# Four-block conditioned transformer stack: loops written out, and three small moves in the 16-head attention stages

## The chip, the cores and the metric

One NeuronCore of one Trainium2 chip runs the whole program, with one launch. The metric is the device time of an execution in microseconds (us); lower is better. The engines are named as in the profile: PE (TensorE, with PEld for its weight loads), DVE (VectorE), ACT (ScalarE), POOL (GpSimd) and SP (SyncE, which issues most DMAs).

## The reference

The input x has 64 sequences of 64 tokens with 256 features, 4096 tokens in all. Four blocks change it one after the other; each takes its shifts, scales and gates from a condition vector of the sequence. All is computed in fp32.

```python
# block 0: layer norm, 16 heads of 64, gelu MLP of 1024
# block 1: rms norm, 16 heads of 16 with q/k rms norm and 3-D rope, SwiGLU of 682
# block 2: layer norm, 16 heads of 16 with rope by position, gelu MLP, then a gate unit
# block 3: two low-rank products per sequence, with gelu between
h = norm(x) * (1 + scale_a) + shift_a
q, k, v = heads(h @ Wqkv)
q, k = rope(qk_norm(q), qk_norm(k))        # block 1; block 2 without the norm
x = x + gate_a * (softmax(q @ k.T / sqrt(d)) @ v @ Wo + bo)
h = norm(x) * (1 + scale_m) + shift_m
x = x + gate_m * mlp(h)
```

## The kernel before, in words

x stays in SBUF as X, features on the partitions. The tokens go through every stage in NCH = 8 chunks of 512. The stages, each a block of its own with a barrier at its end, are: attention0 (block 0, 64 features a head), feed_forward, attention12 (block 1), feed_forward, attention12 (block 2), feed_forward, the gate unit (feed_forward again, kind "gate") and low_rank.

A large product is three fp32r products (`split3`): the weights and the activations are each held as a rounded high half and the rest as a low half. For activations, ACT writes the high half HH from H32 (`act_hh`, line 298), and DVE the low half HL = H32 - HH (`dve_hl`, line 396). For weights of the next stage, ACT and mostly POOL do the same during the last two chunks (`wt.high`, `wt.low`, line 206; two pieces a step in attention12).

`Front` makes the normed and modulated chunk H32. In attention12 this runs ahead: in body c it works on chunk c + 2 (`early`). Its pieces there are: a square on ACT and a sum XS of it on POOL (`pool_ss`, line 314) in step 1; high and low part of that sum in step 2 (`act_sqh`; `pool_sql`, line 318, writes FB); variance on PE (`pe_var`, line 338, reads FB), its root and DVE's Newton steps in step 3, with POOL's scale and shift (`pool_h`, lines 325 and 332); the high half in the tail.

attention12 has no scheduler. The order of each engine is that of its own `step` function, called by `steps`: body c runs step t = 1, 2, 3 of chunk c and then step 0 of chunk c + 1 as its tail. A step handles 128 tokens, tile tt = 4c + t, and looks ahead: the projection to q and k is made for tile tt + 2 (`pe_proj`, line 1413), the rotation by POOL for tile tt + 2 (`pool_rope`, lines 1508 to 1513), the transposes of q and k for tile tt + 1 (`qk_t`, line 1556), the weighted sum for tile tt - 1. In block 1 the q/k norm lies between: ACT squares the projection (`act_square`, line 1435), DVE sums (`dve_sum`, line 1466), ACT takes the root (`act_root`, lines 1440 and 1442), DVE multiplies (`dve_qk`, line 1483). ACT also copies the transposed softmax weights out of two PSUM banks (lines 1686 to 1689, PT); the first of these banks is the one that `qk_t` writes next, so `qk_t` waits for the first copy.

Before the change, ACT takes the root of tile tt + 2 ahead of the two copies in steps 1, 2 and 3, and behind them in step 0 only. DVE makes the low half of chunk c + 1 in step 1 of body c, behind `spread_k` (line 1735); PE needs it in step 2, whose projection is the first of chunk c + 1. In body 0 (`lead`) the low half of chunk 1 stands at the end of step 1. The projected result is scaled by the gate into RT or RTa (line 1745), and POOL adds it to X two bodies later (`add`, line 1816), in the tail behind the rotation.

Loops: `chunks` runs bodies 0 to 5 as a hardware loop of three turns with two bodies each (line 441), the last two straight; `steps` of attention12 runs body 0 straight, 1 to 4 in a loop of two turns (line 1527), and 5 to 7 straight. The gate unit is straight already. In a loop, semaphore values and addresses that depend on c come from registers.

## Time and profile before

| | before |
|---|---|
| median of 3 runs | 2075.79 us (2071.45 to 2076.36) |
| profiled execution, its time | 2075.19 us |
| its span in the trace | 2073.4 us |
| mean granted TensorE clock | 0.968 |
| PE busy | 1872.6 us (90%) |
| DVE, ACT, POOL busy | 1380.5, 1028.9, 799.0 us |

The stages end at about 619.4, 836.1, 1150, 1380, 1670, 1880, 2036 and 2073.4 us of the span, in the order above. Busy time is time in which an instruction runs on the engine; waits and register instructions are not in it. The granted clock is a share of TensorE's full speed. In rows in order of time, "x2" is a row of two merged instructions, and a bracket gives the idle time of the engine before it and what ended it.

### The profile page before, as it was taken

The page shows a single profiled execution, that of the slowest core. Times are in us where ns is not written, and L with a number is a line of the kernel's source. Part 1 is how long each engine was busy: PE and PEld are TensorE (multiplying, and loading weights), DVE is VectorE, ACT ScalarE, POOL GpSimd, SP SyncE. Part 2 cuts the span into 40 slices and gives each one's busy share as a digit, 9 for nine tenths or more (in the row PEclk, how much of TensorE's full clock was granted, in tenths as well). Part 3 has the DMA queues.
Part 4 walks back from the last instruction along what each step waited for, and adds up shares of the span by engine and source line. Part 5 has one row for each costly group of instructions (what it writes and reads, how often), then busy time and mean ns, then how long its engine had stood idle before and what let it go on. Part 6 is the DMA issues. An engine that isn't in the chain of part 4 may idle for free. (4 is left out here: it accounts for less than half of the span.)

```text
span 2073.4 us, 42326 instructions
## 1 busy us (share of the span) xinstructions
PE 1872.6 (90%) x16038; PEld 1464.3 (71%) x16038; DVE 1380.5 (67%) x2128; ACT 1028.9 (50%) x1793; POOL 799.0 (39%) x737
## 2 busy tenths in 40 slices
PE   5999999999979998688988899978999889998998
PEld 4778777877867776466766677756777677776775
DVE  4665666566655665588898577767889756664555
ACT  3544444444447665366666344324555556663332
POOL 1210211021123445557668233446777824450000
PEclk8999999999989999799999999989999999999999
DMA  5100000000010000100000000010000000003322
GB/s 187 72 2 2 2 2 2 2 2 2 2 50 13 0 0 1 46 2 3 2 2 2 28 0 0 0 41 2 2 0 2 2 31 0 0 1 91 107 77 82
DMA packets 26596, 44.58 MB, mean 22 GB/s; under 512 B 4289, under 2 KB 12289, under 8 KB 26305
## 3 DMA queue, kind: packets, MB, share of 16 engines
q1 hardware_dynamic: 25152, 42.01, 6.1%
q8 instruction: 123, 2.02, 0.4%
q10 hardware_dynamic: 1280, 0.23, 0.1%
q14 instruction: 41, 0.33, 0.1%
HBM read 35.94 MB, written 6.29 MB: 20 GB/s over the span
## 5 line engine op out<-in xcount | busy, mean ns | idle before, releaser
L1230 DVE TENSOR_TENSOR Glb<-Gfb,Ghb 128x512 fp32r<-128x512 f32 x176 | 155.7, 894 | 67.0 <-ACT Ghb L1181 65.3
L449 PE MATMUL bank<-HH,W1b 128*128 128x512 f32 x448 | 184.8, 413 | 16.0 <-PEq L1538 7.1
L325 POOL TENSOR_TENSOR Tm<-Dv,MOD 128x512 f32<-128x512 f32 x94 | 108.4, 1173 | 204.6 <-DVE Dv L388 128.9
L451 PE MATMUL bank<-HH,W1b 128*128 128x512 f32 x448 | 177.2, 396 | 0.0
L450 PE MATMUL bank<-HL,W1b 128*128 128x512 f32 x448 | 177.0, 395 | 0.0
L449 PE MATMUL O<-Ghb,W2b 128*128 128x512 f32 x352 | 141.0, 400 | 31.7 <-DVE Glb L1230 31.6
L469 POOL TENSOR_TENSOR spare<-RT 128x1 f32<-128x1 f32 x32 | 11.4, 355 | 397.9 <-DVE RT L460 397.9
L314 POOL TENSOR_TENSOR XS<-Tm 128x512 f32<-128x512 f32 x48 | 70.1, 1460 | 214.5 <-ACT Tm L280 209.6
L451 PE MATMUL O<-Ghb,W2b 128*128 128x512 f32 x352 | 138.0, 392 | 0.0
L450 PE MATMUL O<-Glb,W2b 128*128 128x512 f32 x352 | 137.6, 391 | 0.0
L669 DVE COPY VP<-bank 64x256 f32<-64x256 f32 x128 | 54.0, 422 | 114.0 <-PE bank L632 112.7
L1413 PE MATMUL bank<-WQKa,HH 128*128 128x512 f32 x256 | 91.0, 438 | 41.0 <-DVE HL L396 17.9
L1689 ACT ACTIVATE PTa<-bank 128x512 f32<-128x512 f32 x128 | 69.4, 593 | 98.4 <-PE bank L1569 98.4
L449 PEld LDWEIGHTS bank<-HH,W1b 128*128 128x128 f32 x448 | 85.8, 191 | 41.4 <-issue 17.8
L1180 ACT ACTIVATE Gfb<-bank,bias_cols 128x512 f32<-128x512 f32 x128 | 88.0, 688 | 51.0 <-DVE Glb L1230 40.9
L449 PE MATMUL bank<-HH,WQK 128*128 128x512 f32 x256 | 107.4, 420 | 4.6 <-DVE HL L396 4.6
L449 PEld LDWEIGHTS O<-Ghb,W2b 128*128 128x128 f32 x352 | 66.3, 188 | 56.1 <-DVE Glb L1230 43.0
L332 POOL TENSOR_TENSOR H<-Tm,MOD 128x512 f32<-128x512 f32 x94 | 98.5, 1069 | 11.8 <-POOL Tm L325 10.6
L450 PE MATMUL bank<-HL,WQK 128*128 128x512 f32 x256 | 101.5, 396 | 0.0
L451 PE MATMUL bank<-HH,WQK 128*128 128x512 f32 x256 | 101.4, 396 | 0.0
L632 PE MATMUL bank<-WV,HH 128*128 128x256 f32 x512 | 98.7, 286 | 2.7 <-DVE WV L206 2.7
L450 PEld LDWEIGHTS bank<-HL,W1b 128*128 128x128 f32 x448 | 86.0, 192 | 20.8 <-issue 3.3
(266 smaller groups left out, 5278.2 us busy)
## 6 DMA issues: line engine op xcount, KB each, us to landing
w<-l_w_dram SPq DMA_DIRECT2D x33, 256.0 KB, 3.4
X<-xT_dram SPq DMA_DIRECT2D x16, 256.0 KB, 6.7
out_dram<-XO SPq DMA_DIRECT2D x8, 512.0 KB, 2.7
wm<-w_mods_dram SPq DMA_DIRECT2D x4, 768.0 KB, 5.0
W2b_f<-l_w_dram SPq DMA_DIRECT2D x11, 256.0 KB, 5.2
WQK_f<-l_wqk_dram SPq DMA_DIRECT2D x8, 256.0 KB, 7.3
W1b_0f<-l_w_dram SPq DMA_DIRECT2D x8, 256.0 KB, 3.6
wm<-w_mods_dram SPq DMA_DIRECT2D x4, 384.0 KB, 6.7
```

Of the source, the lines that this page charges most:

```text
L314: nc.gpsimd.tensor_tensor(XS[:], Tm[:, 0], Tm[:, 1], ALU.add).then_inc(f_ss.h, 1)
L325: nc.gpsimd.tensor_tensor(Tm[:, k].rearrange("p (b t) -> p b t", t=T), Dv[:, k].rearrange("p (b t) -> p b t", t=T), m, ALU.mult).then_inc( ...
L332: last = nc.gpsimd.tensor_tensor(H32[p][:, k].rearrange("p (b t) -> p b t", t=T), Tm[:, k].rearrange("p (b t) -> p b t", t=T), m, ALU.add)
L449: nc.tensor.matmul(out, w_lo_ap, x_hi, start=first, stop=False)
L450: nc.tensor.matmul(out, w_hi_ap, x_lo, start=False, stop=False)
L451: return nc.tensor.matmul(out, w_hi_ap, x_hi, start=False, stop=last)
L632: last = nc.tensor.matmul(out, (HH, HL)[xp][p][:, k, tok_], WV[wp][:, k, :, jj * DH0:(jj + 2) * DH0], start=(k == 0 and wp == 1), stop=(k ...
L669: last = nc.vector.tensor_copy(v_dst(jj, 1, a, b), v_src(1, a, b))
L1180: nc.scalar.activation(Gf[m % 2][:], src, ACT.Gelu, bias=bias(0, m))
L1230: nc.vector.tensor_tensor(Gl[m % gb][:], gf, Gh[m % gb][:].bitcast(F32), ALU.subtract).then_inc(g_lo.h, 1)
L1413: last = nc.tensor.matmul(QKB[:], (HH, HL)[xp][p][:, k, t * P:(t + 1) * P], WQK[wp][:, k], start=(i == 0 and k == 0), stop=(i == 2 and k = ...
L1689: nc.scalar.activation(PT[:, 4 * i:4 * i + 4].rearrange("p r q -> p (r q)"), bank[:], ACT.Copy).then_inc(pt_sb.h, 1)
```

## The change

It has four parts. (1) All loops are written out: `chunks` and `steps` no longer take the engine, and call the body eight times with constants. (2) In both attention12 stages the low half of a chunk is made by POOL, in the tail step, behind the rotation (`pool_hl`), from body 0 on for chunk c + 2; DVE keeps only the one of chunk 1 in body 0. (3) POOL's add to X moves from the tail to the next step, step 1, behind its rotation; only the add of the last tail stays. (4) In block 1 ACT takes the root in step 1 behind the two copies, as it did in step 0.

```diff
+            def pool_hl(self, pool, c, p):
+                pool.wait_ge(f_hh.h, self.at(f_hh, c + 1))
+                nc.gpsimd.tensor_tensor(HL[p][:], H32[p][:], HH[p][:].bitcast(F32), ALU.subtract).then_inc(f_hl.h, 1)
...
-        def chunks(eng, body, unrolled=False):
-
-            if unrolled:
-                for c in range(NCH):
-                    body(c, c % 2, 2 if c < NCH - 2 else NCH - 1 - c)
-                return
-            with eng.Fori(0, NCH // 2 - 1) as j:
-                body(2 * j, 0, 2)
-                body(2 * j + 1, 1, 2)
-            body(NCH - 2, 0, 1)
-            body(NCH - 1, 1, 0)
+        def chunks(body):
+
+            for c in range(NCH):
+                body(c, c % 2, 2 if c < NCH - 2 else NCH - 1 - c)
...
-                    body(0, 0, 2)
-                    with eng.Fori(0, NCH // 2 - 2) as j:
-                        body(2 * j + 1, 1, 2)
-                        body(2 * j + 2, 0, 2)
-                    body(NCH - 3, 1, 2)
-                    body(NCH - 2, 0, 1)
-                    body(NCH - 1, 1, 0)
+                    for c in range(NCH):
+                        body(c, c % 2, 2 if c < NCH - 2 else NCH - 1 - c)
...
                             if ahead(t, more, tail, 2):
                                 act_square(act, tt + 2)
-                                if t != 0:
+                                if t > 1:
                                     act_root(act, tt + 2)
...
-                            if ahead(t, more, tail, 2) and t == 0:
+                            if ahead(t, more, tail, 2) and t < 2:
                                 act_root(act, tt + 2)
...
-                            if t == 1 and not lead:
-                                lf.dve_hl(dve, lc, lp)
...
-                            if tail and past(tt, 2 * TL):
+                            if tail and more:
+                                f.pool_hl(pool, cc, 1 - p)
+                            if (t == 1 or tail and not more) and past(tt, 2 * TL):
                                 add(c - 2, p)
                             if t == 1:
                                 f.pool_ss(pool, cc)
```

POOL's order in block 1's attention, from the end of the tail's rotation over step 1: before (a straight body; QNa, RAa, RBa are the rotation's tiles, X the residual stream, XS the sum of squares of the front).

```order
L1513 TENSOR_TENSOR QNa_6798<-RAa_6800,RBa_6801 128x32x12
L1816 TENSOR_TENSOR X<-X,RT 128x2x512
L1508 TENSOR_TENSOR RAa_6800<-QNa_6799,TWa1c 128x32x12
L1510 TENSOR_TENSOR RBa_6801<-QNa_6799,TWa1s 128x32x6 x2
L1510 TENSOR_TENSOR QNa_6799<-QNa_6799,W4a_214 128x16x4
L1513 TENSOR_TENSOR QNa_6799<-RAa_6800,RBa_6801 128x32x12
L314 TENSOR_TENSOR XS<-Tm 128x512
```

The same place now:

```order
L1510 TENSOR_TENSOR QNa_10998<-RAa_11000,RBa_11001 128x32x12
L400 TENSOR_TENSOR HL_191<-H_1_187,HH_189 128x1024
L1505 TENSOR_TENSOR RAa_11000<-QNa_10999,TWa1c 128x32x12
L1507 TENSOR_TENSOR RBa_11001<-QNa_10999,TWa1s 128x32x6 x2
L1507 TENSOR_TENSOR QNa_10999<-QNa_10999,W4a_214 128x16x4
L1510 TENSOR_TENSOR QNa_10999<-RAa_11000,RBa_11001 128x32x12
L1806 TENSOR_TENSOR X<-X,RT 128x2x512
L314 TENSOR_TENSOR XS<-Tm 128x512
```

The low half HL has the place that the add to X had, and the add stands one rotation later, ahead of the sum of squares.

ACT's order at the start of step 1 in block 1's attention, before (SQa square of the projection, SSa root, PTa weights' copies, QTa and KBa q and k out of the transposes; HH is the end of the tail):

```order
L298 ACTIVATE HH_189<-H_1_187 128x1024
L1435 ACTIVATE SQa_6796<-bank 128x512
L1440 ACTIVATE SSa_6797<-SSa_6797,spare 128x32
L1442 ACTIVATE SSa_6797<-SSa_6797 128x32
L1689 ACTIVATE PTa_6808<-bank 128x512 x2
L1672 ACTIVATE QTa_6802<-bank 128x256
```

And now:

```order
L298 ACTIVATE HH_188<-H_0_186 128x1024
L1432 ACTIVATE SQa_10996<-bank 128x512
L1681 ACTIVATE PTa_11008<-bank 128x512 x2
L1437 ACTIVATE SSa_10997<-SSa_10997,spare 128x32
L1439 ACTIVATE SSa_10997<-SSa_10997 128x32
L1664 ACTIVATE QTa_11002<-bank 128x256
```

The two copies stand directly behind the square, and the root, which waits for DVE's sum, behind them.

## Rows read from the trace of the kernel before

**Rows 1.** The page: whole program, then busy us and share of the span by engine.

```profile
span 2073.4 us, 42326 instructions
...
PE 1872.6 (90%) x16038; PEld 1464.3 (71%) x16038; DVE 1380.5 (67%) x2128; ACT 1028.9 (50%) x1793; POOL 799.0 (39%) x737
```

**Rows 2.** Busy time by stretch: span, then busy us by engine, granted clock, DMA.

```profile
836.10:1150.00 313.90, 261.31 (x2960) 201.28 (x2960) 258.70 (x464) 189.33 (x404) 204.49 (x227) 0.94 0.03 9
210.78:281.45 70.67, 69.29 (x862) 57.31 (x863) 42.55 (x73) 33.52 (x64) 11.70 (x10) 0.98 0.01 2
281.45:349.42 67.97, 63.96 (x780) 52.36 (x778) 42.45 (x74) 32.04 (x61) 11.71 (x10) 1.00 0.01 2
349.42:418.19 68.77, 67.66 (x862) 56.03 (x863) 42.55 (x74) 33.44 (x64) 11.75 (x10) 1.00 0.01 2
941.03:1014.17 73.14, 63.16 (x740) 48.45 (x740) 63.41 (x117) 46.01 (x99) 48.22 (x55) 0.98 0.01 2
1050.30:1086.10 35.80, 30.62 (x371) 23.80 (x371) 32.22 (x59) 22.81 (x50) 24.26 (x28) 1.00 0.01 2
1472.43:1505.34 32.91, 31.57 (x376) 24.30 (x375) 29.18 (x48) 17.47 (x33) 25.53 (x24) 1.00 0.01 2
```

**Rows 3.** Waits of PE: total us, times, longest.

```profile
PE bank L1556 <- ACT PTa L1689: 26.8, 37, 4.1
PE bank L1413 <- DVE HL L396: 17.9, 12, 7.7
...
PE S L754 <- issue: 4.2, 2, 2.2
```

**Rows 4.** In order of time, block 1's step 1: start, us, engine, line, operation.

```profile
1045.66 1.31 POOL L1510 TENSOR_TENSOR RBa<-QNa,TWa1s 128x192 f32<-128x192 f32 x2
...
1047.75 0.58 ACT L1435 ACTIVATE SQa<-bank 128x512 f32<-128x512 f32 x1
...
1049.09 0.32 ACT L1440 ACTIVATE SSa<-SSa,spare 128x32 f32<-128x32 f32 x1 [0.76 <-DVE SSa L1466]
...
1049.58 1.07 ACT L1689 ACTIVATE PTa<-bank 128x512 f32<-128x512 f32 x2
...
1050.30 0.63 PE L1556 MATMUL bank<-ident,QNa 128*128 128x128 f32 x4 [1.83 <-ACT PTa L1689]
...
1052.90 2.35 POOL L1510 TENSOR_TENSOR RBa<-QNa,TWa1s 128x192 f32<-128x192 f32 x2
...
1053.49 1.21 DVE L396 TENSOR_TENSOR HL<-H,HH 128x1024 fp32r<-128x1024 f32 x1
...
1054.24 1.04 ACT L280 ACTIVATE Tm<-X 128x1024 f32<-128x1024 f32 x1
...
1054.76 0.73 PE L1413 MATMUL bank<-WQKa,HH 128*128 128x512 f32 x2 [0.55 <-DVE HL L396]
...
1056.45 0.60 ACT L1435 ACTIVATE SQa<-bank 128x512 f32<-128x512 f32 x1 [1.17 <-PE bank L1413]
```

**Rows 5.** In order of time, block 2's steps 1 to 3 of one chunk.

```profile
1505.15 2.37 POOL L1816 TENSOR_TENSOR X<-X,RTa 128x1024 f32 x1
...
1509.97 0.73 PE L1413 MATMUL bank<-WQKa,HH 128*128 128x512 f32 x2 [0.75 <-DVE HL L396]
...
1514.62 1.27 POOL L1508 TENSOR_TENSOR RAa<-QNa,RCa 128x512 f32<-128x512 f32 x1 [0.93 <-DVE QNa L1485]
...
1518.59 1.28 POOL L318 TENSOR_TENSOR FB<-XS,FA 128x512 fp32r<-128x512 f32 x1
...
1521.06 0.47 PE L338 MATMUL O<-FB,mean_w 128*128 128x512 f32 x1
```

**Rows 6.** In order of time, block 2's chunk 6 and into chunk 7.

```profile
1612.22 2.51 POOL L206 TENSOR_TENSOR W1b<-W1b_0f,W1b 128x512 fp32r<-128x512 f32 x2
...
1620.10 0.47 PE L338 MATMUL O<-FB,mean_w 128*128 128x512 f32 x1 [0.30 <-issue]
...
1642.31 3.49 POOL L206 TENSOR_TENSOR W2b<-W2b_f,W2b 128x512 fp32r<-128x512 f32 x2
```

More of the change, by code:

```diff
@@ L825, in _ @@
                         mod_transposes(pe, 2)
-                        chunks(pe, steps(step, lambda c: None))
+                        chunks(steps(step, lambda c: None))
                     @block.scalar
@@ L895, in _ @@
                         st.weights.high(act, 4)
-                        chunks(act, steps(step, lambda c: None))
+                        chunks(steps(step, lambda c: None))
                     @block.vector
@@ L1004, in _ @@
                         dve.wait_ge(x_in[2].h, x_in[2].at(16 * DH * (NCH - 2)))
-                        chunks(dve, steps(step, residual))
+                        chunks(steps(step, residual))
                         step_v.pending = step_c.n[0]
@@ L1035, in body @@
                             residual_pool(pool, c)
-                        chunks(pool, body)
+                        chunks(body)
                 d_in.passed(16 * n_small); step_v.passed(step_v.pending)
@@ L1165, in body @@
                                     f.pe_mean(pe, cc)
-                        chunks(pe, body, gate)
+                        chunks(body)
                     @block.scalar
@@ L1209, in body @@
                                     wt.high(act, 1)
-                        chunks(act, body, gate)
+                        chunks(body)
                     @block.vector
@@ L1269, in body @@
                                 residual_dve(dve, c, l, G_M, bcol_out, O2)
-                        chunks(dve, body, gate)
+                        chunks(body)
                     @block.gpsimd
@@ L1294, in _ @@
                         if not gate:
-                            chunks(pool, body)
+                            chunks(body)
                 if not gate:
@@ L1517, in ahead, with steps @@
                     return more >= 1 if tail else t + n < TL or more >= 1
-                def steps(eng, step):
+                def steps(step):
                     def body(c, p, more):
@@ L1653, in _ @@
                         step(0, 0, 0, 2, first=True)
-                        steps(pe, step)
+                        steps(step)
                         out_t(pe, NT - 1)
@@ L1721, in _ @@
                         step(0, 0, 0, 2, first=True)
-                        steps(act, step)
+                        steps(step)
                         oh(NT - 1, 1)
@@ L1799, in _ @@
                         fr.dve_norm(dve, 1)
-                        steps(dve, step)
+                        steps(step)
                         for tt in (NT - 2, NT - 1):
@@ L1835, in _ @@
                         step(0, 0, 0, 2, first=True)
-                        steps(pool, step)
+                        steps(step)
                         add(NCH - 1, 1)
```

## The prediction

> **What bounds the kernel now.** I read the page's busy times first, then each engine's busy time by stage and by chunk, then the PE waits, and last the instructions of single steps in order of time. PE is busy 1872.6 us of 2073.4 [rows 1], so what is to be had lies in its idle 200.8 us. "Chunk" is one loop body of 512 tokens; a 16-head stage makes four steps of it, here called steps 1, 2, 3 and 0 (the tail). In the 16-head stage of block 1, PE idles 52.6 of 313.9 us while DVE is busy 258.7 [rows 2]. A straight chunk of it (the one from 1050.30) takes 35.80 us with PE at 30.62 and DVE at 32.22: part of each chunk hangs on DVE and on what ACT does for it. In block 2's, a chunk of 32.91 us has PE at 31.57: PE is the bound, little is left. The PE waits that bear on the edits are three [rows 3]: for ACT's copy of the weights (26.8 us, 37 times), for DVE's low half (17.9 us, 12 times), and "issue" before the 64-head scores (4.2 us, 2 times), which come right behind loop back edges. The sum is made against the profiled execution, 2075.2 us; the median of the runs shown, 2075.8, is 0.6 above it. 0.3%, which is 6.2 us, is about what a measurement of this kernel can tell from no change.
>
> **Loops written out.** Ten back edges are taken: two in each of the four looped stages with a count of 3, one in each 16-head stage. Where one costs, the chunk around it is long: 70.67 us with the first and 68.77 with the second of stage one, 67.97 between them [rows 2], so 2.7 and 0.8. The first also has a granted clock of 0.98, so some of the 2.7 is matmuls at 1.2 instead of 2.4 GHz behind the gap. In block 1's attention the two chunks with the back edge take 73.14 against twice 35.80: 1.5. The list of PE waits shows no "issue" of 2 us or more for the other seven, so I give them 0. Sum 5.0 us; bounds: 0, if the next wait would have taken the time anyway, and 6.7, the 4.2 of rows 3 and about 2.5 left for block 1. The register instructions that go too (semaphore values and addresses) are costed at nothing: the straight chunk of 35.80 is no shorter than the looped ones.
>
> **Root behind the copies, step 1, block 1 only.** ACT squares the projection at 1047.75, then its root waits for DVE's sum until 1049.09, and only then come the copies at 1049.58, for which PE waited 1.83 us at 1050.30 [rows 4]. With the root behind, the first copy can start at the end of the square, 1048.33; it takes half of 1.07, so PE goes on at about 1049.0: 1.3 us earlier. The root itself ends some 0.2 us later; DVE, which needs it next, is busy with its maximum until about then, so this costs up to 0.2.
>
> **Low half from DVE to GpSimd.** DVE loses 1.21 us per chunk [rows 4]. GpSimd gains one subtraction of 128x1024. The nearest rows: 2.37 for its add of the same size, 2.51 for two low halves of 512, 3.49 for two others that met DVE's work [rows 5, 6]. I take 2.4, as GpSimd does it in the slot that the add to x has today; 3.49 is kept for the range. The wait for the high half holds up what is queued behind it on GpSimd, the next rotation; but that rotation waits for DVE's product of the next step in any case; it starts at 1507.5 today and would then [rows 5]. At 1054.76 PE waited 0.55 for the low half; that goes. Both edits would give PE 1.85 us a chunk. But the next square at 1056.45 can't move ahead of the one for the mean, which ends at 1055.28 (1054.24 and 1.04): ACT allows 1.2. The same two rows in the other chunks give 1.2 to 2.0, so I take 1.3, for chunks 1 to 5: 6.5 us; bounds 0.5 (only the low half's wait goes) and 2.0. Chunk 0 is not touched: there DVE keeps the low half, and PE waits for it later whatever ACT does.
>
> What the row at 1052.90 shows is against the obvious fear. GpSimd's two products take 2.35 us beside DVE's low half, and 1.31 at 1045.66 [rows 4]: the two engines hold each other up, and taking the subtraction off DVE gives GpSimd about 1.0 back. The Trainium skill (Perfetto Trace Analysis, Optimizing Scalar/DVE Operations) says the opposite lesson of the same fact: the two share an SBUF port, so moving work between them might not help. By the trace I count the move as a gain; by that sentence it gives nothing, and this is the first rival.
>
> **Residual a step later.** In block 2's step 1 today GpSimd adds at 1505.15 (2.37), rotates, sums the squares, rotates at 1514.62, and its last piece for the variance starts at 1518.59, is done at 1519.87, and PE takes it at 1521.06 [rows 5]. Now: low half to 1507.5; rotation of 4.0 (1.0 less, as above) to 1511.5; add to 1513.9; sum 1.28 to 1515.2; rotation to 1519.2; the piece to 1520.5. PE, without its wait of 0.75 at 1509.97, wants it at 1520.3. So 0.25 of the 0.75 comes back: 0.5 a chunk, 2.5 us for chunks 1 to 5. The add itself is waited for two steps further on, so it costs nothing; that cover holds up to several us.
>
> In the last chunks GpSimd also makes low halves of the next stage's weights, two a step. In block 2's chunk 6 two of them (2.51, from 1612.22 [rows 6]) stand in this very run of work and leave GpSimd no pause: of the 2.4 for the low half only the 1.0 of the shorter rotation is made up. The piece comes 1.4 later, PE stalls where it now goes on at 1620.10, and what GpSimd does up to the end of the stage moves along: 1.35 us lost. In block 1's chunk 6 the same leaves 0.5 of the gain, and in chunk 7, with the added 2.4 in front of the variance, I reckon 1.2 lost.
>
> **Sum:** 5.0 + 6.5 + 2.5 + 0.5 - 1.2 - 1.35 = 11.95, so 12 us: 2075.2 - 12 = 2063 us. The feed-forward stages only lose their loops: 0.
>
> **Rivals.**
> 1. The offload gives nothing, because GpSimd's added work holds DVE up as long as the subtraction did. Then block 2's 2.5 and 0.5 in each of five chunks go: about 7 us gained, 2068. For it: the two engines do stretch each other. Against: DVE's products read PSUM for the most part. 0.15.
> 2. More than I count: 2.0 a chunk in seven chunks of block 1 (14), 0.75 in six of block 2 (4.5), back edges 5, no loss at the ends: 23.5, so 2052 to 2054. For it: gaps of 1.8 us vanish, and with them some stretches at 1.2 GHz. 0.20.
> 3. Half of it is not seen: PE gains in step 1, then waits the same for DVE in steps 3 and 0, where DVE's Newton work is the bound; left are some back edges and the losses at the ends. About 3 us gained, 2072. 0.12.
> 4. Slower. GpSimd becomes late in each step 3, at the variance. If low half and add take 3.5 each (as at 1642.31 [rows 6]) instead of 2.4, 2.2 us come on top. Block 2: the piece at 1522.7 against PE's 1521.06, 1.7 lost in five chunks (8.3), 3.6 in chunk 6; block 1: 0.5 gained in five chunks (2.5), 1.7 and 3.4 lost in the last two; back edges 5.0 gained. Sum 9.5 us slower, 2084.5. It decides from where the two together take 2 us more than the 4.8 I give them. Against: the add takes 2.37 beside other DVE work now [rows 5]. 0.05.
>
> **How the numbers follow.** Forecast 2063 with 0.48. The cases reach from 2052 to 2084.5; leaving out the slower one and the edges of 2 and 3, the range is 2054 to 2071. Faster by over 0.3% means under 2069.6: the forecast, rival 2 and two thirds of rival 1, 0.78. Within it: rival 3 and the rest of rival 1, 0.17. Slower 0.05.
>
> **What would show it.** In block 1 the wait of 1.8 us before the transposes of step 1 falls to about 0.5 and chunks take 34.5 us, not 35.8; the first 64-head chunks take 68 us each; no "issue" wait of 2 us is left. In block 2 no wait for a low half from chunk 1 on, and PE waits 0.2 to 0.3 before the variance, over 1 in chunk 6. GpSimd's low half takes 2.4 us. I am wrong if chunks of block 1 stay above 35.3, if the straight code shows new "issue" waits, or if PE waits for GpSimd by more than 0.5 in every chunk.

## The result, and the profile after

The changed kernel takes **2044.8 us** (median of 4 runs, 2043.4 to 2046.8); the kernel before, beside it, 2073.6. The ratio is 0.9865, 95% interval 0.9851 to 0.988: 28.9 us gained, where I had forecast 12. Two later sessions gave the same code 2046.8 and 2047.9 us against 2074.1 and 2074.8. The sign was right, the size less than half.

The head of its page, against [rows 1]:

```profile
span 2041.6 us, 40224 instructions
...
PE 1851.9 (91%) x16038; PEld 1451.6 (71%) x16038; DVE 1367.6 (67%) x2114; ACT 1017.5 (50%) x1787; POOL 820.8 (40%) x751
```

The same 16038 matmuls are busy 1851.9 us, not 1872.6. So of the 31.8 us between the two spans, 20.7 stand in PE's *busy* time and only 11.1 in its idle time. The mean granted clock goes with it: 0.976, where it was 0.968. Between the levels of 2.4 and 1.2 GHz that makes 133 us at the lower one before (6.4% of 2073.4) and 98 after (4.8% of 2041.6). 35 us less at half speed are, by my estimate, about 17 us of matmul time. One such place: before, PE idles 2.2 us ahead of the scores at 211.1, and the granted clock of 212.3 to 215.7 is 0.50; in the changed kernel the wait is gone and the clock is 1.00 throughout these chunks. A gap that goes can take slow matmuls behind it along, and I had priced gaps alone, with one exception.

Every stage ends at a barrier of all engines, whose time the trace has (block 1's feed-forward ended at 1375.1 us before, not at about 1380). Stage by stage, in the profiled executions:

| stage | before | after | change | my forecast |
|---|---|---|---|---|
| 64-head attention | 619.4 | 615.6 | -3.8 | -3.5 |
| block 0 feed-forward | 216.7 | 214.5 | -2.2 | 0 |
| block 1 attention | 314.0 | 307.6 | -6.4 | -7.3 |
| block 1 feed-forward | 225.0 | 214.9 | **-10.1** | 0 |
| block 2 attention | 295.5 | 290.7 | -4.8 | -1.15 |
| block 2 feed-forward | 206.8 | 204.4 | -2.4 | 0 |
| what follows | 196.0 | 193.9 | -2.1 | 0 |

The same changed code in two more executions had 614.1 and 614.7, 305.8 and 305.7, 219.0 and 219.0, and 292.2 and 289.9 us in the first, third, fourth and fifth row. So a difference of 2 us in one stage, and of 4 in block 1's feed-forward, is no finding by itself; the lengths of plain chunks repeat better, mostly to 0.05 us, and carry most readings below.

Busy time by stretch (span; then PE, its weight loads, DVE, ACT and GpSimd; granted clock; DMA), first of the kernel before, block 1's feed-forward and block 2's attention:

```profile
1150.10:1375.10 225.00, 211.25 (x888) 167.64 (x888) 160.96 (x210) 83.97 (x109) 85.64 (x78) 0.98 0.02 7
1375.10:1670.60 295.50, 262.82 (x2992) 201.14 (x2992) 236.90 (x376) 145.34 (x273) 213.97 (x192) 0.96 0.03 8
```

and of the changed kernel, two first chunks of the 64-head stage, block 1's two stages and block 2's attention:

```profile
207.00:274.80 67.80, 65.78 (x822) 54.20 (x821) 42.45 (x73) 32.75 (x62) 11.73 (x10) 1.00 0.01 2
274.80:342.60 67.80, 65.79 (x822) 54.20 (x821) 42.45 (x73) 32.74 (x62) 11.73 (x10) 1.00 0.01 2
...
830.10:1137.70 307.60, 253.94 (x2960) 196.13 (x2960) 259.98 (x457) 185.94 (x404) 213.81 (x234) 0.96 0.03 9
1137.70:1352.60 214.90, 207.59 (x888) 166.95 (x888) 161.97 (x210) 81.52 (x107) 87.64 (x78) 0.99 0.02 7
1352.60:1643.30 290.70, 260.79 (x2992) 200.77 (x2992) 222.95 (x369) 144.90 (x273) 223.96 (x199) 0.96 0.03 9
```

All 64-head chunks are now 67.80 us, also those that took 70.67 and 68.77 [rows 2]. The waits of PE that answer to [rows 3] (total us, times, longest):

```profile
PE O L446 <- DVE Glb L1227: 24.3, 19, 1.8
PE bank L1548 <- ACT PTa L1681: 21.3, 37, 1.6
PE bank L1410 <- DVE HL L396: 15.9, 2, 8.2
```

The "issue" wait before the 64-head scores is gone from the list. The low half is waited for twice, in the first chunks that the change leaves alone, not 12 times. The wait for DVE's Glb (Ghb and Glb are the high and low half of the hidden layer), in the three feed-forward stages together, is 24.3 us in 19 times where before's list has 31.6 in 24: a row that I had read past, since none of the three moves touches those stages.

Block 1's step 1 in order of time, answering [rows 4]:

```profile
1034.95 0.58 ACT L1432 ACTIVATE SQa<-bank 128x512 f32<-128x512 f32 x1
1035.39 2.36 POOL L400 TENSOR_TENSOR HL<-H,HH 128x1024 fp32r<-128x1024 f32 x1
1035.43 1.06 ACT L1681 ACTIVATE PTa<-bank 128x512 f32<-128x512 f32 x2
...
1036.15 0.63 PE L1548 MATMUL bank<-ident,QNa 128*128 128x128 f32 x4 [0.48 <-ACT PTa L1681]
...
1036.39 0.32 ACT L1437 ACTIVATE SSa<-SSa,spare 128x32 f32<-128x32 f32 x1
...
1040.04 1.35 POOL L1507 TENSOR_TENSOR RBa<-QNa,TWa1s 128x192 f32<-128x192 f32 x2
...
1041.37 1.05 ACT L280 ACTIVATE Tm<-X 128x1024 f32<-128x1024 f32 x1
```

The copies follow the square at once, PE waits 0.48 us instead of 1.83, GpSimd's low half takes 2.36, and its two products are back at 1.35 from 2.35. Block 2, a plain chunk and then what bears on [rows 6]:

```profile
1479.73 2.37 POOL L400 TENSOR_TENSOR HL<-H,HH 128x1024 fp32r<-128x1024 f32 x1
...
1486.10 2.37 POOL L1806 TENSOR_TENSOR X<-X,RTa 128x1024 f32<-128x1024 f32 x1
...
1493.69 1.28 POOL L318 TENSOR_TENSOR FB<-XS,FA 128x512 fp32r<-128x512 f32 x1
...
1495.07 0.47 PE L338 MATMUL O<-FB,mean_w 128*128 128x512 f32 x1
...
1593.51 0.47 PE L338 MATMUL O<-FB,mean_w 128*128 128x512 f32 x1 [2.18 <-issue]
1601.65 0.63 PE L1548 MATMUL bank<-ident,QNa 128*128 128x128 f32 x4 [0.34 <-ACT PTa L1681]
1613.51 0.66 PE L1548 MATMUL bank<-ident,QNa 128*128 128x128 f32 x4 [2.72 <-POOL QNa L1510]
```

FB is done at 1494.97 and PE takes it at 1495.07, without a wait. In chunk 6, where GpSimd makes weights' low halves as well, PE waits 2.18 us at the variance and then 2.72 for the rotation.

### The profile page after: what moved, and what is told of

Read it like the earlier page. It is cut to its first block and busy times, and to the rows that moved or that the text cites. A ratio compares the mean times of both kernels' runs of the same rounds, so it can differ in the third digit from the quotient of the medians.

```text
span 2041.6 us, 40224 instructions
## 1 busy us (share of the span) xinstructions
PE 1851.9 (91%) x16038; PEld 1451.6 (71%) x16038; DVE 1367.6 (67%) x2114; ACT 1017.5 (50%) x1787; POOL 820.8 (40%) x751
## 5 line engine op out<-in xcount | busy, mean ns | idle before, releaser
L446 PE MATMUL O<-Ghb,W2b 128*128 128x512 f32 x352 | 140.8, 400 | 24.5 <-DVE Glb L1227 24.3
L1690 ACT ACTIVATE SPa<-SPa 128x1024 f32<-128x1024 f32 x64 | 68.2, 1066 | 66.2 <-DVE SPa L1759 65.8
L1753 DVE TENSOR_REDUCE mxa<-S 128x16 f32<-128x1024 f32 x64 | 78.0, 1218 | 34.5 <-PE S L1612 33.9
```

The source lines that it names most:

```text
L446: nc.tensor.matmul(out, w_lo_ap, x_hi, start=first, stop=False)
L1753: nc.vector.tensor_reduce(mx[:, t % 2], sv, AXX, ALU.max).then_inc(s_max.h, 1)
```

## Experiments

Sixteen runs. "Chunk" times are from one matmul on FB (L338) to the next; for each kind I give the plain one. Totals are medians, ratios are against the kernel before of the same session. The median of the kernel before differs by up to 2.7 us between sessions, so across sessions it is the ratios that compare.

### Loops and moves taken apart

`loops_only` is the kernel before with every loop written out:

```
-            if unrolled:
+            if True:
...
-                    body(0, 0, 2)
-                    with eng.Fori(0, NCH // 2 - 2) as j:
...
+                    for c in range(NCH):
+                        body(c, c % 2, 2 if c < NCH - 2 else NCH - 1 - c)
```

> The kernel before with every loop written out and none of the three moves. Theory A (the moves matter in the 16-head stages alone, written-out code everywhere else): the 64-head stage and the three feed-forward stages take their time of the changed kernel (615.6, 214.5, 214.9 and 204.4 us), block 1's attention loses only its back edge (314.0 to about 312.5) and block 2's nothing (295.5); some 20 to 22 us gained, 2051 to 2054 us. Rival B (the written-out code also shortens the 16-head chunks, the moves give nothing): block 1's attention near 307.6, block 2's near 290.7, 2044 to 2047 us. Rival C (my forecast's own working): feed-forward stages as before, 5 us gained, 2068 us.

`moves_only` is the changed kernel with the loops back (in the 16-head stages over chunks 2 to 5, since the add to x now starts in chunk 2):

> The changed kernel with the loops put back (one back edge an engine in each 16-head stage, two in each other looped stage): the three moves alone. Theory A: only the two 16-head stages get shorter, block 1's by about 5 us (chunks of 34.4 instead of 35.6 us, less what the last two give back), block 2's by 3 to 5; 2064 to 2067 us, and the feed-forward stages keep 216.7, 225.0 and 206.8. Rival B (the moves give nothing): 2072 to 2075 us. Rival C (my forecast's working for the moves): 7 us gained, 2066 to 2067, of it 6.5 in block 1 and 1.2 in block 2: told from A by block 2's stage alone.

Measured: loops_only 2056.7 us, ratio 0.9918 (0.9889 to 0.9948), so 17 us gained; moves_only 2065.5, ratio 0.9962 (0.9947 to 0.9978), 8 us gained. The two add up to about 25 of the 27 to 29. Stages and plain chunks:

| | block 0 ff | block 1 att. | chunk | block 1 ff | chunks | block 2 att. | chunk | block 2 ff |
|---|---|---|---|---|---|---|---|---|
| before | 216.7 | 314.0 | 35.60 | 225.0 | 25.93, 26.53 | 295.5 | 32.90 | 206.8 |
| moves_only | 216.8 | 312.8 | 34.44 | 225.9 | 25.94, 26.50 | 288.5 | 31.95 | 206.6 |
| loops_only | 214.8 | 309.6 | 35.70 | 219.0 | 25.15 | 292.8 | 32.66 | 205.5 |
| after | 214.5 | 307.6 | 34.44 | 214.9 | 25.17 | 290.7 | 31.92 | 204.4 |

Theory A holds in its outline: the moves act in the 16-head stages alone, 1.2 us a chunk in block 1 and 0.75 in block 2 (0.95 with the loops in); written-out code does the rest. Its number for the total of loops_only was 3 us too low, and "nothing" for loops in block 2 was wrong (0.25 a chunk). The total of moves_only came as theory A said, the stages did not: block 1's is only 1.2 us shorter where about 5 was expected, and block 2's 7.0 where it was 3 to 5. Block 1's chunks are as short as expected, but the one that now holds the loop's back edge took 38.5 us. TensorE's branch instruction lasted 3.6 us there, and PE idled behind it:

```profile
PE bank L1417 <- issue: 2.7, 1, 2.7
```

The granted clock of that chunk was 0.91, against 1.00 in the one before. In block 2 the moves gained 7.0 us with the loops in and 2.1 without them (292.8 to 290.7). Most of the difference lies in the last chunk: 37.4 fell to 34.4 us with the loops in, 36.3 became 36.7 without them. Why is open.

My own working for the moves priced block 1's chunk well. Its zero for the feed-forward stages fell. The length of the branches is in the trace of the kernel before, first `chunks`, then the 16-head stages (ns min/median/max):

```profile
L441 PEldq COMPARE_BRANCH  x12: 76/214/3803, 206.7 to 1827.0; - x12
L1527 PEldq COMPARE_BRANCH  x4: 76/160/3317, 969.6 to 1564.6; - x4
```

Three of the ten back edges took 3.3 to 3.8 us, the two of the 64-head stage and the one of block 1's attention. The other seven took 0.21 to 0.24 us each, 1.6 in all, so their branches can't be what the feed-forward stages lost.

### Why written-out code helps a stage that has no long back edge

In the loops of block 1's feed-forward the chunks alternate, 25.93 and 26.53. ACT in order of time, kernel before:

```profile
1234.22 1.28 ACT L289 ACT_TABLE_LOAD   x1
1235.51 0.64 ACT L292 ACTIVATE V<-V 128x512 f32<-128x512 f32 x1
1236.18 0.63 ACT L294 ACTIVATE V<-V 128x512 f32<-128x512 f32 x1
1238.17 1.28 ACT L1177 ACT_TABLE_LOAD   x1 [1.36 <-PE bank L451]
1239.46 0.60 ACT L1177 ACTIVATE Gfb<-bank 128x512 f32<-128x512 f32 x1
```

and the same place in the changed kernel:

```profile
1217.82 1.28 ACT L289 ACT_TABLE_LOAD   x1
1219.12 0.63 ACT L292 ACTIVATE V<-V 128x512 f32<-128x512 f32 x1
1219.78 0.64 ACT L294 ACTIVATE V<-V 128x512 f32<-128x512 f32 x1
1220.43 1.28 ACT L1174 ACT_TABLE_LOAD   x1
1221.79 0.60 ACT L1174 ACTIVATE Gfb<-bank 128x512 f32<-128x512 f32 x1
```

ACT goes from the root's functions to Silu and loads its table. In the loop ACT waits for PE first, on a count that sits in a register, and then loads: the trace has the wait at a register instruction of its own (ALU_OP, 1238.1). In straight code the wait is on a constant and stands at the activation itself, so the load runs while PE is still at work. The load is worth 1.28 us in ACT's chain; that chain ends in the Glb that PE waits for. Three runs test it:

`load_ahead`, the kernel before and one line:

```
                                 if f and f.norm and m == M_RSTD:
                                     f.act_rstd(act, cc)
+                                    nc.scalar.preload_act_table_set(...)
```

> The kernel before, loops kept, and in the looped feed-forward stages ACT loads the table of Gelu or Silu right behind the root, ahead of its wait for TensorE. Theory L (what the loops cost these stages is this load of 1.28 us, which stood behind the wait): block 1's feed-forward falls from 225.0 to 216 or less, the other two by 1 to 2 us each, 10 to 13 us in all, 2061 to 2064 us. Rival R (the register instructions and back edges themselves cost it): less than 2 us gained, 2072 to 2074 us, and block 1's feed-forward chunks stay at 25.9 and 26.5 us.

`load_behind`, the changed kernel with the load tied to the wait:

```
                                 act.wait_ge(a_ps.h, a_ps.at(g + 1))
+                                if not gate and m == M_RSTD + 1:
+                                    nc.scalar.preload_act_table_set(...)
                                 act.wait_ge(g_lo.h, g_lo.at(g - 1))
```

> The changed kernel, straight code, with the same load put behind the wait for TensorE in these stages, as it stood in the loops. Theory L: the feed-forward stages go back to about 216.5, 224 and 206.5 us, so 11 to 13 us slower than the changed kernel, 2056 to 2058 us. Rival R: less than 2 us slower, 2045 to 2047 us, and block 1's feed-forward chunks stay at 25.17 us.

Measured: load_ahead 2072.6 us, ratio 0.9994 (0.9979 to 1.0009); load_behind 2049.7 in the session where no changed kernel ran. Neither number of theory L came; the total of load_ahead is that of rival R, but not for R's reason, since chunks moved. They move as theory L says, only by less: in load_ahead those of 25.93 become 25.48 and those of 26.53 stay at 26.49; in load_behind those of 25.17 become 25.61. So the load behind the wait costs 0.44 us a chunk in block 1, in the loop only in every other chunk. In the two Gelu stages it costs nothing: 25.83 stays 25.83, and 25.61 stays 25.62.

What makes every other chunk 1 us longer showed in a count. ACT's groups in block 1's feed-forward, kernel before:

```profile
L1177 ACT ACT_TABLE_LOAD x11 | 14.1, 1283 | 22.6 <-PE bank L451 22.4
L289 ACT ACT_TABLE_LOAD x8 | 10.3, 1283 | 0.1
```

Eleven loads for eight chunks: one behind each of the eight roots, and one at the head of each of the loop's three passes, the first of which any code needs. The idle time before them has to be taken apart: 9.5 us are the start of the stage, 8.8 the wait for PE at the heads of the second and third pass, and 4.1 are three loads that stand behind their wait (1.36 each), one in the second chunk of each pass. The other five follow the root within 0.1 us. In the trace of load_ahead the load at the head takes the first 1.28 us of ACT's work in the chunks of 26.49. `load_both` adds a load ahead of the loop, so that Silu's table is loaded on both ways into a pass, from ahead of the loop and from the pass before:

```
+                        if not gate:
+                            nc.scalar.preload_act_table_set(...)
                         chunks(act, body, gate)
```

> The kernel before, loops kept; in the looped feed-forward stages ACT loads the table of Gelu or Silu right behind the root, as in the run that did that alone, and once more ahead of the loop, so that the load at the head of each pass goes (it stood there three times a stage). Theory L (in block 1's feed-forward the loop costs what these loads cost): the chunks of 26.49 us with the loop's head fall to 25.3 to 25.5 like the others, the stage from 222.7 to 218 to 220 us; 2066 to 2069 us in all. Rival R (the branch and the register instructions make those chunks long): they stay at 26.4 or more and the stage at 222 to 223 us.

Its groups and its stretch of the same stage:

```profile
L1195 ACT ACT_TABLE_LOAD x8 | 10.3, 1283 | 0.1
L1212 ACT ACT_TABLE_LOAD x1 | 1.3, 1283 | 4.7 <-PEq L1541 4.7
...
1154.10:1372.10 218.00, 208.92 (x888) 167.63 (x888) 162.41 (x210) 81.50 (x107) 85.99 (x78) 0.99 0.02 7
```

Measured: the long chunks fall from 26.49 to 25.58, the stage from 225.0 to 218.0 with all its loops; the whole 2070.7 us, ratio 0.9969 (0.9959 to 0.998), so 6 us gained (I had expected 2066 to 2069 us). Theory L holds for the chunks: 0.45 us in three and 0.95 in two, and the two loads at the later heads are gone. Of the stage's 7 us 2.9 are the fall of its last chunk (28.15 to 25.22), which a section below shows to be a toss-up of each execution. The Trainium skill (ScalarE: Activation LUTs, What ACT_TABLE_LOAD costs) gives about 1283 ns for the load and about 2.66 us for a switch with its drain. The load agrees; load and activation start only 1.36 us apart here, so 1.3 is the price by this trace.

`moves_loads` puts the three moves, the loops and these loads together:

> The three moves, the loops kept, and in the looped feed-forward stages the loads of Gelu's or Silu's table right behind the root and ahead of the loop. Theory A (of the loops' cost about 7 us are these loads, the rest are back edges in the 64-head stage and block 1 and 0.2 us a chunk): 2065.5 of the run with the moves alone less 6 to 7, 2058 to 2061 us. Rival B (table loads explain all of it): 2050 us or less. Rival C (they give nothing once the moves are there): 2064 us or more.

Measured 2060.3 us, ratio 0.993 (0.9903 to 0.9957): theory A's number, 5 us below the moves alone, though the two intervals overlap a little. Block 1's feed-forward takes 220.5 us here, with the toss-up lost; against 225.0 before and 219.0 for straight code that also lost it, the loads are 4.5 of 6 us. By its five plain chunks, which no toss-up touches, they are 3.2 of 5.0: 130.8 us before, 127.6 here and 125.8 in straight code. The rest of the way to 2046 needs straight code: 64-head chunks of 67.8 us throughout, 0.2 us in each chunk of the Gelu stages (25.83 to 25.61), and block 1's attention, where the chunk with the back edge took 38.4 us here again.

### Which move does what

Each is the changed kernel with one move undone: `no_root` (the root of step 1 ahead of the copies), `no_hl` (low half on DVE at the old place), `no_add` (add to x back in the tail, behind GpSimd's low half).

```
-                                if t > 1:
+                                if t != 0:
...
+                            if t == 1 and not lead:
+                                lf.dve_hl(dve, lc, lp)
...
-                            if (t == 1 or tail and not more) and past(tt, 2 * TL):
+                            if tail and past(tt, 2 * TL):
```

> The changed kernel with the root of step 1 back in front of the copies. Theory A (root and low half both count, as in the forecast: 1.83 us and 0.55 us of PE's wait): block 1's attention chunks go from 34.44 back to 35.1 to 35.7 us, its stage is 4 to 7 us longer, block 2 is unchanged; 2048 to 2052 us. Rival B (the low half on GpSimd alone makes the gain): chunks stay below 34.7 us, less than 1.5 us slower.

> The changed kernel with the low half back on DVE at the old place, the add to x still in step 1. Theory A: block 1's chunks 34.9 to 35.2 us (PE's 0.55 comes back), block 2's go from 31.92 to 32.6 (0.75 comes back), and the last two chunks of block 1 (36.65 and 36.08) lose what they gave up, about 1.5 us: 4 to 6 us slower in all, 2049 to 2051 us. Rival B (root alone makes block 1's gain): block 1's chunks stay at 34.4 to 34.6, block 2's alone get longer: 1 to 2.5 us slower.

> The changed kernel with the add to x back in the tail, behind GpSimd's low half: GpSimd has 4.8 us to do before the next rotation. Theory A (the add had to leave the tail, because rotation and sum of squares would come late): block 2's chunks 32.5 to 34 us instead of 31.92, block 1's over 35; 2050 to 2060 us. Rival B (GpSimd has the time): both kinds of chunk stay within 0.2 us, and the last chunks of block 1 get up to 1.7 us shorter: 2043 to 2046 us.

| | total | ratio | block 1 att. | chunk | block 2 att. | chunk | chunks 6 and 7 |
|---|---|---|---|---|---|---|---|
| after | 2044.8 | 0.9865 | 307.6 | 34.44 | 290.7 | 31.92 | 34.19, 36.68 |
| no_root | 2051.0 | 0.9875 | 311.9 | 35.10 | 290.6 | 31.94 | 34.15, 36.63 |
| no_hl | 2051.2 | 0.9874 | 312.1 | 35.42 | 287.8 | 32.00 | 33.34, 33.03 |
| no_add | 2067.4 | 0.9956 | 321.9 | 36.5, 38.1 | 296.6 | 32.63 | 34.55, 39.92 |

The kernel before, measured beside these three, took 2076.3 us, and the changed kernel was not run beside them. By the ratios no_root and no_hl can't be told from the changed kernel in the whole; the readings rest on the chunks. In block 1, undoing the root costs 0.65 us a chunk, as theory A said (35.1 to 35.7), and undoing the low half 1.0, which is more than it said (35.42 against 34.9 to 35.2). Block 2 came out against both theories for no_hl. Its chunk does not change when DVE makes the low half again, and the last two chunks get 4.5 us shorter. The 0.75 that PE waited there [rows 5] was not cured by GpSimd but by the add's leaving. DVE's low half in block 2's attention (ns min/median/max), before, in loops_only, and in no_hl, which in block 2 differs from loops_only by the add's move alone:

```profile
L396 DVE TENSOR_TENSOR HL<-H,HH x7: 1695/2070/2233, 1406.7 to 1606.5; 128x1024 fp32r<-128x1024 f32 x7
L396 DVE TENSOR_TENSOR HL<-H,HH x7: 1215/1866/2160, 1424.6 to 1623.6; 128x1024 fp32r<-128x1024 f32 x7
L396 DVE TENSOR_TENSOR HL<-H,HH x7: 1214/1217/1811, 1431.1 to 1627.9; 128x1024 fp32r<-128x1024 f32 x7
```

Beside GpSimd's add it took 2.07 us (1.87 in loops_only), without it 1.22, and the wait for it is gone from block 2's plain chunks: 32.66 us in loops_only, 32.00 in no_hl.

no_add is the costly one, about 19 us longer than the changed kernel by the ratios and only 9 below the kernel before; theory A had expected 2050 to 2060. Low half and add stand in one slot, 4.7 us. In block 1's attention PE then waits 15 times for DVE's QNa, where in the changed kernel it is 10 times (11.1 us), and in block 2, from 1390 to 1620 us, it waits five times for GpSimd's rotation, where in the changed kernel it is once (2.7 us):

```profile
PE bank L1548 <- ACT PTa L1681: 18.1, 21, 2.7
PE bank L1410 <- DVE QNa L1480: 16.6, 15, 2.4
...
PE bank L1548 <- POOL QNa L1510: 5.4, 5, 1.1
```

The low half on GpSimd is only good with the add moved; the add's move alone is what block 2 wants.

### The same code again, and a copy held by memsets

> The changed kernel, unaltered, once more, so that the variants beside it are compared in one session, and to see which stages repeat. Expected 2043 to 2047 us; if the 2.0 us in the last chunk of block 1's feed-forward (25.20 us here, 27.5 to 28.2 where DVE's copy to Ghb takes 2.77 us beside GpSimd's zeroing of VBa) are a toss-up of each execution and no property of the code, it may come back with 27 us there and up to 3 us more in all.

> The changed kernel, unaltered, for a comparison within one session: 2043 to 2048 us. The last chunk of block 1's feed-forward either 25.2 or 27.3 us; both came up with this same code.

Measured 2046.8 and 2047.9 us, and both times block 1's feed-forward took 219.0 us, not 214.9. The last chunk in the second execution (GpSimd, DVE, PE):

```profile
1339.96 1.50 POOL L318 TENSOR_TENSOR FB<-XS,FA 128x512 fp32r<-128x512 f32 x1 [0.74 <-ACT FA L285]
...
1340.93 2.77 DVE L1225 CAST Ghb<-Gfb 128x512 fp32r<-128x512 f32 x1
...
1341.40 2.02 POOL L1342 MEMSET VBa<- 128x544 f32 x4
...
1344.48 0.50 PE L446 MATMUL O<-Ghb,W2b 128*128 128x512 f32 x1 [2.85 <-DVE Glb L1227]
```

and in the first:

```profile
1341.89 1.49 POOL L318 TENSOR_TENSOR FB<-XS,FA 128x512 fp32r<-128x512 f32 x1 [0.74 <-ACT FA L285]
...
1342.86 0.80 DVE L1225 CAST Ghb<-Gfb 128x512 fp32r<-128x512 f32 x1
...
1343.32 2.31 POOL L1342 MEMSET VBa<- 128x544 f32 x4
```

DVE's copy starts 0.47 and 0.46 us ahead of GpSimd's memsets, and once it is done in 0.80 us, once it lasts to their end. The same code, so a toss-up of the execution: 2.0 us directly, and a lower clock behind. Both times GpSimd's subtraction to FB had started 0.97 us ahead of the copy and ended 0.5 us into it. So what is tossed is who goes on when that ends: the copy, and then the first memset is long (0.83 us, not 0.55), or all four memsets in a row. Of the eighteen traces the copy won in four (the changed kernel's, load_behind, load_both, no_add). It fell well in the profiled execution of the changed kernel, and 4 of the 10.1 us there are owed to that; 6 are the change's. `fills_early` moves the memsets, and the rotation's tables that GpSimd makes behind them for block 1, to the head of the last chunk's work, in loops_only:

> The kernel before with written-out loops and none of the moves, and in the feed-forward stages GpSimd zeroes VBa at the head of the last chunk's work, not near its end. Theory M (DVE's copy to Ghb is held up by those memsets, 2.77 us instead of 0.8, and PE waits 2.8 us for what follows): block 1's last feed-forward chunk falls from 27.52 to 25.2 to 25.6 us, the stage from 219.0 to about 216.7. Rival N (the copy waits for something else): the chunk stays at 27 us or more and the copy takes 2.7 us.

Measured 2060.8 us, ratio 0.9925 (0.9905 to 0.9946), so no faster than loops_only (0.9918), and not clearly slower; the copy of 2.77 us is gone from its old place and one of 3.21 us stands beside GpSimd's add to X and the memsets at the new one. Theory M's mechanism holds, its cure does not: the chunk is 27.26, and block 0's last full chunk, 23.6 elsewhere, is 29.63 at a granted clock of 0.83: there 8 us of fills now stand ahead of GpSimd's work for the next chunk, and PE waits 6.4 us for a Glb. The Trainium skill (SBUF — State Buffer, SBUF: two separate sides) says that one port pair is shared by DVE and GpSimd and held for a whole instruction by whichever starts first, the other being fully blocked. The trace agrees: GpSimd's subtraction started first both times, and the copy ends 0.28 us behind what held it up, the subtraction (1343.38) or the last of the four memsets (1343.42). Who goes on when the first starter is done, neither that section nor these runs tell in advance.

### Versions built on this

`best1` gives GpSimd the low half in block 1 only and not in its last chunk; `best2` also makes the first chunk's low half earlier on DVE. `best4` is the changed kernel with block 2's low halves on DVE and nothing else, `best3` adds the earlier one in block 2:

```
+                            if t == 1 and l != 1:
+                                lf.dve_hl(dve, lc, lp)
...
-                            if t == 1 and lead:
+                            if t == 1 and lead and l == 1:
                                 lf.dve_hl(dve, lc, lp)
...
-                            if tail and more:
+                            if tail and more and l == 1:
                                 f.pool_hl(pool, cc, 1 - p)
```

This is best3's edit; best4 lacks its middle part and has `not lead` in the first.

> The changed kernel, but the low half goes to GpSimd in block 1 alone and there not in the last chunk; in block 2, and in that chunk, DVE makes it as before. Theory A (in block 2 the whole gain is the add's, and GpSimd's low half only costs, in the last two chunks): block 2's attention 287.8 us as in the run with DVE's low half, against 290.6; block 1's last chunk of steps about 2 us shorter (its idle time 6.6 instead of 9.0): 4 to 5 us faster than the changed kernel, 2039 to 2042 us. Rival B (the losses at the ends come from the granted clock and the add): within 1 us of the changed kernel.

> As the one beside it, and in the first chunk of both 16-head stages DVE makes the low half right behind its share of K, not at the end of the step, where PE waits 7.7 us for it in block 2. By the trace it can start at 1382.5 instead of 1383.9, so 1.4 us less wait in block 2 and up to that in block 1: 2036 to 2040 us. Rival: the outputs' reciprocal and division, now behind it, come later and PE waits for them instead; no change against the one beside it.

> The changed kernel with block 2's low halves back on DVE (behind its share of K, as before the change), block 1 untouched. Theory A: block 2's attention 287 us instead of 290.6 to 292.2, everything else as in the changed kernel: 3 to 5 us faster than the changed kernel beside it. Rival B (what is saved there comes back as time at the lower clock, in the stages behind it): within 1.5 us of it.

> As best4, and in block 2's first chunk DVE makes the low half right behind its share of K, not at the end of the step. Theory A: block 2's attention 285.5 us, 1.5 us below best4, so 5 to 6.5 us faster than the changed kernel. Rival B: as above, within 1.5 us of it.

| | total | changed kernel beside it | block 1 att. | block 2 att. |
|---|---|---|---|---|
| best1 | 2048.2 | 2046.8 | 309.8 | 287.0 |
| best2 | 2047.6 | 2046.8 | 309.7 | 285.4 |
| best4 | 2045.4 | 2047.9 | 306.3 | 286.5 |
| best3 | 2044.4 | 2047.9 | 307.6 | 283.1 |

Block 2's attention does what theory A says in all four:

```profile
1356.40:1639.50 283.10, 257.99 (x2992) 198.75 (x2992) 230.85 (x376) 144.97 (x273) 214.30 (x192) 0.98 0.03 9
```

Less of it arrives in the whole. best1 and best2 missed theory A's totals (2039 to 2042 and 2036 to 2040). They lose it in block 1, where the last chunk is 0.8 us shorter but what follows it takes 15.5 us instead of 12.6, at a granted clock of 0.73 instead of 1.00. best4 and best3 come out 2.6 and 3.5 us below the changed kernel, where theory A had 3 to 5 and 5 to 6.5; their ratios against the kernel before, 0.9855 and 0.9854, both with 0.9832 to 0.9877, overlap the changed kernel's 0.9864 (0.984 to 0.9888). best3 is the fastest that I ran in its session, by an amount that four runs each don't settle.

## Why the prediction was right or wrong

- **Loops written out, the back edges.** Right where I looked: 3.5 forecast and 3.8 measured in the 64-head stage, 67.80 us a chunk. In block 1's attention 1.5 was forecast; loops_only is 4.4 below before there: 2.2 in the two long chunks (37.54 and 36.09 to 35.70 each), 2.3 ahead of the first variance, a stretch that took 47.7 to 49.7 us in three executions of one code. But the whole term was 5.0 us, and loops_only measured 17; the three moves had 7 and measured 8.
- **"I give them 0" for the seven other back edges, and "register instructions at nothing".** This is the step that failed. In the feed-forward stages it hid 14.7 us of the profiled 31.8. (Four of these the toss-up gave.) The branches at these seven were indeed short, 0.21 to 0.24 us each. The largest cost that the runs trace is what ACT's table loads do in a loop: one behind the wait, one more at the head of each pass, 3.2 of the 5.0 us in block 1's plain feed-forward chunks. What I took for proof, that the straight chunk of block 1's attention is no shorter, was true (35.70 against 35.60) and told nothing of stages where ACT changes tables. The rows to see it were there: in block 1's feed-forward 11 loads for 8 chunks, three of them behind a wait, and 7.2 us of PE waiting for Glb, which became 2.4. The cause of the rest stays open: 0.35 us in each of block 1's plain chunks, 0.2 in each Gelu chunk, where it stands in PE's wait for Glb (1.5 against 1.3 us), and 0.25 in block 2's attention, where it stands in the wait for the low half (0.75 against 0.55).
- **Root behind the copies.** Right: 1.83 to 0.48 us, GpSimd's low half at 2.37 against 2.4, the products back at 1.35. Root and low half together gave 1.26 a chunk (35.70 to 34.44) where I took 1.3; undoing one of them alone costs 0.65 or 1.0. That the whole stage came out at 6.4 against 7.3 is luck, though: the loops gave 4.4 of it where I had 1.5, and the moves only 2.0 (309.6 to 307.6) where I had 5.8, because the ends lost more and the stretch ahead of the first variance fell badly.
- **Residual a step later.** Forecast 0.5 a chunk, measured 0.74 (32.66 to 31.92); FB comes just in time and not 0.25 late. But I had credited the low half's move with the end of the wait of 0.75, and only asked of the add whether it fits. It was the add that made DVE's low half long; no_hl shows that GpSimd's part is nil in block 2.
- **The ends.** Chunk 6 of block 2 lost 0.96 (33.23 to 34.19) against 1.35 forecast, PE waiting 2.18 at the variance as described. In block 1 chunk 6 kept nothing of the gain (36.53 to 36.65) where I had 0.5, and the last chunk grew from 34.35 to 36.08, 1.7 against 1.2.
- **The clock.** I priced it once. Of the measured gain about 17 us are, by the estimate above, matmuls that ran at the higher level. No run separates what the change gave of this from what differs between executions.
- **Rivals.** Rival 1, that the offload gives nothing, is right in block 2 and wrong in block 1: DVE is busy 259.98 of 307.6 us there and 222.95 of 290.7 in block 2. Rival 2 was the nearest in size but put its 23.5 us in the 16-head stages and the back edges, where about 15 of the 31.8 were. Rival 4 did not come: low half and add took 2.37 us each. GpSimd is late at the variance in the last chunks alone (1.1 us in block 1's chunk 6, 2.2 in block 2's), and when the add goes back (no_add), which costs most of the gain, PE's added waits are at the projection and the transposes.

## What to carry to other kernels

When a loop is written out, look beyond branches: count the table loads in a pass and see whether each stands ahead of its wait; here two added lines took 3.2 us out of five chunks with the loops kept, though not all that written-out code gave. When a wait is for an instruction that takes longer than its shape needs, look at what runs beside it: moving the neighbour can cure it for nothing, and moving the instruction itself may only shift the load. Price a gap on TensorE with the slower matmuls behind it, and run the same code twice before a saved microsecond in one stage is believed.

## What the runs showed of the hardware that I had not expected

- A table load (1283 ns, every one of them) ran ahead of a wait for a constant and behind a wait for a register's value, and a loop's head got one of its own: 11 loads against 9 in a stage of 8 chunks.
- Of ten taken back edges TensorE's branch lasted 3.3 to 3.8 us at three and 0.21 to 0.24 at seven. What tells them apart is open.
- DVE's copy of 128x512 takes 0.43 us alone. Started while GpSimd's subtraction runs, with four memsets behind that, it takes 0.80 or 2.77, with the same code and, to 0.01 us, the same starts relative to each other.
- TensorE's mean granted clock was 0.976, 0.974 and 0.973 in three executions of one program. Block 1's feed-forward took 214.9, 219.0 and 219.0 us in them, and a saving of 3 to 5 us in one stage came out as 2.6, 3.5 or nothing in the whole.
